# A mixture-of-experts layer on one core: the expert loop written out, new table steps, a second z3T buffer and a reordered last stage

## The reference, cut to what matters

```python
h = gelu(x[:, 1:] @ W1 + x[:, :1] @ W2 + b)          # 16 x 255 rows of 256
h = h + attention(layernorm(h))                       # 16 heads of 64
z = layernorm(h)
probs = softmax(z @ router_w);  topw, topi = top_k(probs, 2)      # 8 experts
routed = sum over the two experts e of  topw * (silu(z @ w1[e]) @ w2[e])
shared = sigmoid(z @ gate_w) * ((silu(z @ gate) * (z @ up)) @ down)
out = h + routed + shared
```

## Time and profile before

| | us |
|---|---|
| median of 3 runs | 1132.4 (1131.16 to 1133.53) |
| the profiled execution | 1139.81 |
| its span | 1138.0 |
| PE busy in the span | 1062.1 |
| DVE busy | 768.7 |
| POOL busy | 537.2 |

### The profile page before, as it was taken

How to read it: one execution, slowest core, us unless ns; L and a number is a source line. 1 busy time by engine, 2 the same in 40 slices (tenths; PEclk the granted TensorE clock), 3 DMA queues, 4 the chain that set the end, 5 groups by cost and what they waited for, 6 DMA issues and landing times.

```text
span 1138.0 us, 24005 instructions
## 1 busy us (share of the span) xinstructions
PE 1062.1 (93%) x8058; PEld 891.3 (78%) x8059; DVE 768.7 (68%) x1975; ACT 671.1 (59%) x2062; POOL 537.2 (47%) x575
## 2 busy tenths in 40 slices
PE   7979999999999999999999999999979798899985
PEld 6857788878877887877788788788858687898874
DVE  3757766785776678577667857766765954566666
ACT  4647765774775677477567747766774333454431
POOL 0025434554556455464545546454361746544542
PEclk9989999999999999999999999999999988999997
DMA  8110000000001000000100000010025423343494
GB/s 259 56 43 2 1 1 19 2 11 30 20 2 38 20 1 13 27 20 2 38 20 1 20 20 20 1 39 20 2 98 194 134 70 108 112 134 121 131 330 141
DMA packets 46624, 66.07 MB, mean 58 GB/s; under 512 B 7992, under 2 KB 39608, under 8 KB 45496
## 3 DMA queue, kind: packets, MB, share of 16 engines
q1 hardware_dynamic: 39720, 46.73, 13.1%
q0 software_dynamic: 6528, 17.97, 4.3%
q10 hardware_dynamic: 272, 0.00, 0.0%
HBM read 36.22 MB, written 28.46 MB: 57 GB/s over the span
## 4 chain that ended last, share of the span: by engine, by line
PE 72%; DVE 8%; issue 6%; POOL 5%; ACT 2%; another core or an unknown queue 1%; DMA 0%; DVEq 0%; SPq 0%; ACTq 0%; POOLq 0%
PE pT_ps L730 10%; PE o_ps L743 9%; PE proj_ps L68 9%; PE proj_ps L70 9%; PE proj_ps L69 9%; PE s_ps L716 8%; PE v_ps L68 2%; POOL prob L1676 2%; PE v_ps L69 2%; PE v_ps L70 2%; PE s_ps L68 2%; POOL prob L1678 2%; PE s_ps L70 2%; PE pT_ps L977 2%; PE s_ps L69 2%
## 5 line engine op out<-in xcount | busy, mean ns | idle before, releaser
L1039 ACT ACTIVATE prob<-s_ps,nmax 128x255 f32<-128x255 f32 x512 | 239.1, 478 | 227.7 <-DVE nmax L1251 227.6
L1676 POOL TENSOR_SCALAR prob<-prob,rinv 128x255 f32<-128x255 f32 x128 | 139.6, 1090 | 373.8 <-DVE rinv L1269 369.4
L1251 DVE TENSOR_REDUCE nmax<-s_ps 128x2 f32<-128x510 f32 x256 | 166.0, 681 | 37.9 <-PE s_ps L716 36.4
L730 PEld LDWEIGHTS pT_ps<-ident,prob 128*128 128x128 f32 x1024 | 109.8, 141 | 60.6 <-issue 49.7
L730 PE MATMUL pT_ps<-ident,prob 128*128 128x128 f32 x1024 | 146.2, 281 | 6.5 <-POOL prob L1678 3.4
L743 PE MATMUL o_ps<-probT,v 128*64 128x256 f32 x1024 | 139.6, 394 | 1.2 <-DVE oT_lo L1282 1.2
L1276 DVE COPY probT<-pT_ps 128x512 f32<-128x512 f32 x128 | 88.4, 691 | 77.0 <-PE pT_ps L730 77.0
L716 PE MATMUL s_ps<-qk_space 64*128 64x256 f32 x1536 | 125.2, 295 | 5.1 <-ACT prob L1039 4.4
L1678 POOL TENSOR_SCALAR prob<-prob,rinv 128x255 f32<-128x255 f32 x128 | 119.1, 931 | 0.0
L716 PEld LDWEIGHTS s_ps<-qk_space 64*128 64x128 f32 x1536 | 98.9, 185 | 21.8 <-issue 8.5
L1771 POOL DMA_INDIRECT expert_out_rows<-yg,y_at x72 | 69.4, 964 | 81.1 <-DVE yg L1581 45.4
(11 more groups left out here) (267 smaller groups left out, 2778.2 us busy)
## 6 DMA issues: line engine op xcount, KB each, us to landing
xg<-expert_in_rows SPq DMA_DIRECT2D x72, 130.0 KB
back<-expert_out_rows SPq DMA_DIRECT2D x8, 1024.0 KB, 9.4
xin<-in_x_dram SPq DMA_DIRECT2D x8, 512.0 KB, 4.4
z_rows<-z SPq DMA_DIRECT2D x8, 512.0 KB, 3.2
z<-z_rows SPq DMA_DIRECT2D x8, 512.0 KB
expert_in_rows<-bo_row SPq DMA_DIRECT2D x16, 128.0 KB
raw_up<-in_L_ffn_w_dram SPq DMA_DIRECT2D x8, 256.0 KB, 5.0
raw_down<-in_L_ffn_w_dram SPq DMA_DIRECT2D x8, 256.0 KB, 6.3
```

Of the source, the lines that this page charges most:

```text
L730: m = pe.transpose(pT_ps[h][:, o:o + P], prob[u_par(i)][:, h, qt, kt * P:(kt + 1) * P], ident[:])
L1039: m = act.activation(prob[u_par(i)][:, h, qt, 1:N], s_ps[h][:, qt * N + 1:(qt + 1) * N], ACT.Exp, bias=nmax[u_par(i)][:, n:n + 1], accum_o ...
L1251: dve.tensor_reduce(nmax[u_par(i)][:, 2 * h:2 * h + 2], s_ps[h][:].rearrange("p (q k) -> p q k", q=2)[:, :, 1:N], AX_X, ALU.max, negate=Tr ...
L1676: pool.tensor_scalar(prob[k][:, 0, 1, 1:N], prob[k][:, 0, 1, 1:N], rinv[k][:, 1:2], None, ALU.mult).then_inc(s_nA1, 1)
```

## The change

- `RUN` = 71 tiles in place of 72, and the whole expert loop is written out on all engines: no `Fori`, every semaphore value is a constant.
- The running sum `ends` (one copy and seven adds, each waiting for the one before) becomes one multiplication by a constant mask of 8x8 and one reduction. The mask `not_behind` is built on DVE at the start of the second stage.
- POOL waits for the tables (`s_table`) before its first `split_lo`. `hidden_split_lo` of groups 1, 2 and 3 moves from POOL to DVE; DVE's order around the tables changes.
- Two buffers for the transposed z3: `transpose_z3(g+1)` stands between the halves of `hidden(g)`, and ACT and DVE follow that order.
- In the last stage POOL no longer adds pairs: DVE adds twice for every group. `add_shared(6)` stands ahead of `add_experts(7)`. All eight `load_back` are issued ahead of the first store.
- PE's wait for `add_shared(3)` moves from before tile 0's turn to before the first `down_rows`.

```diff
+RUN = TOP * ROWS // P + E - 1
...
-        z3T_hi, z3T_lo = (over(n, qkv_at, 2 * part + k * half, [DC, GR], F32R) for k, n in enumerate(("z3T_hi", "z3T_lo")))
+        z3T_hi = [over("z3T_hi0", qkv_at, 2 * part, [DC, GR], F32R), over("z3T_hi1", qkv_at, 4 * part + half, [DC, GR], F32R)]
+        z3T_lo = [over("z3T_lo0", qkv_at, 2 * part + half, [DC, GR], F32R), over("z3T_lo1", at["probT1"], 0, [DC, GR], F32R)]
...
-            def load_x(r, k, first):
-
-                n = UNROLL * r + k
-                if not first:
+            def load_x(n):
+                if n >= BUFS:
                     sp.wait_ge(s_yc, n - BUFS + 1)
-                at = sp.value_load(tile_in[0:1, bass.ds(n, 1)], min_val=0, max_val=E * CAP + (SPARE - 1) * P)
-                sp.dma_start(xg[k % BUFS][:], x_slots[bass.ds(at, P), :]).then_inc(s_x_in[k % BUFS], 16)
-
-            def turn(r, last):
-                for k in range(UNROLL):
-                    if k + BUFS < UNROLL or not last:
-                        load_x(r + (k + BUFS) // UNROLL, (k + BUFS) % UNROLL, False)
+                at = sp.value_load(tile_in[0:1, n:n + 1], min_val=0, max_val=E * CAP + (SPARE - 1) * P)
+                sp.dma_start(xg[n % BUFS][:], x_slots[bass.ds(at, P), :]).then_inc(s_x_in[n % BUFS], 16)
...
-            for k in range(BUFS):
-                load_x(0, k, True)
-            for k in range(UNROLL):
-                load_x((k + BUFS) // UNROLL, (k + BUFS) % UNROLL, False)
-            with sp.Fori(1, TURNS - 1) as r:
-                turn(r, False)
-            turn(TURNS - 1, True)
+            for n in range(RUN):
+                load_x(n)
 
 
             load_z3(SHARED_EARLY + 2)
-            for k in range(UNROLL):
...
-            for g in range(2, 5):
+            for g in range(2, GROUPS):
                 load_back(g)
             for g in range(GROUPS):
                 store_group(g)
-                if g + 5 < GROUPS:
...
                 hidden(g, 0)
-                hidden(g, 1)
                 if g + 1 < SHARED_EARLY:
                     transpose_z3(g + 1)
+                hidden(g, 1)
...
-            transpose_x(0, 0)
-            transpose_x(0, 1)
+            transpose_x(0)
+            transpose_x(1)
             pe.wait_ge(s_table, TABLE_STEPS)
             pe.wait_ge(s_prod, FC * SHARED_EARLY)
-            up(0, 0, experts_of(0, 0)[0])
-            pe.wait_ge(s_added, 2 * SHARED_EARLY)
-            turn(0, True, False)
-            with pe.Fori(1, TURNS - 1) as r:
-                turn(r, False, False)
-            last_expert = turn(TURNS - 1, False, True)
+            e = experts_of(0)
+            up(0, e[0])
+            for n in range(RUN):
+                if n and n % HALF == 0:
+                    e = experts_of(n // HALF)
+                transpose_h(n)
+                if n + 2 < RUN:
+                    transpose_x(n + 2)
+                if n + 1 < RUN:
+                    up(n + 1, e[n + 1])
+                if n == 1:
+                    pe.wait_ge(s_added, 2 * SHARED_EARLY)
+                if n > 0:
+                    down_rows(n - 1, e[n - 1])
 
 
             transpose_z3(SHARED_EARLY)
-            down_rows(TURNS - 1, UNROLL - 1, last_expert)
+            down_rows(RUN - 1, e[RUN - 1])
...
             split_hi(1)
             silu(2, 0)
+            z3_hi(3)
+            hidden_split_hi(2, 0)
+            silu(2, 1)
+            hidden_split_hi(2, 1)
             split_hi(2)
-            silu(2, 1)
-            hidden_split_hi(2, 0)
-            z3_hi(3)
-            hidden_split_hi(2, 1)
+            silu(3, 0)
             split_hi(3)
-            silu(3, 0)
+            hidden_split_hi(3, 0)
             silu(3, 1)
...
-            def gated(r, k, first):
-                n = UNROLL * r + k
+                act.activation(xgT_hi[n % 2][:], xT_ps[n % 2][:, 0:DC * P], ACT.Copy).then_inc(s_xh, 1)
+
+            def gated(n):
                 act.wait_ge(s_up, n + 1)
-                if not first:
+                if n >= 2:
                     act.wait_ge(s_hT, n - 1)
-                act.activation(hg[k % 2][:], hg_ps[k % 2][:, 0:F], ACT.Silu).then_inc(s_h, 1)
-
-            def hidden_hi(r, k, first):
-                n = UNROLL * r + k
+                act.activation(hg[n % 2][:], hg_ps[n % 2][:, 0:F], ACT.Silu).then_inc(s_h, 1)
...
             z3_hi(SHARED_EARLY)
             for g in range(SHARED_EARLY, GROUPS):
                 silu(g, 0)
-                silu(g, 1)
-                hidden_split_hi(g, 0)
                 if g + 1 < GROUPS:
                     z3_hi(g + 1)
+                hidden_split_hi(g, 0)
+                silu(g, 1)
...
-                done(dve.tensor_copy(ends[:, 0:1], tiles_f[0:1, 0:1]))
-                for e in range(1, E):
-                    done(dve.tensor_tensor(ends[:, e:e + 1], ends[:, e - 1:e], tiles_f[0:1, e:e + 1], ALU.add))
+                done(dve.tensor_tensor(upto[:], not_behind[:], tiles_f[0:1].unsqueeze(1).broadcast_to([1, E, E]), ALU.mult))
+                done(dve.tensor_reduce(ends[:], upto[:], AX_X, ALU.add))
...
+            def hidden_split_lo(g):
+                for c in range(FC):
+                    dve.wait_ge(s_hhi, FC * g + c + 1)
+                    dve.tensor_tensor(h_lo[g % 2][:, c, :], h_full[:, c, :], f32(h_hi[g % 2][:, c, :]),
+                                      ALU.subtract).then_inc(s_hlo, 1)
...
+            dve.wait_ge(s_iota, 1)
+            dve.tensor_tensor(not_behind[:], iota[0:1].unsqueeze(2).broadcast_to([1, E, E]),
+                              iota[0:1].unsqueeze(1).broadcast_to([1, E, E]), ALU.is_ge)
...
             expert_ends()
+            dve.wait_ge(s_hlo, FC)
+            hidden_split_lo(1)
+            turns_past()
             add_shared(0)
             product(2, 0)
-            turns_past()
-            product(2, 1)
             z3_lo(3)
             tile_words()
+            product(2, 1)
+            hidden_split_lo(2)
             add_shared(1)
             product(3, 0)
             product(3, 1)
+            hidden_split_lo(3)
             add_shared(2)
             add_shared(3)
 
-            def x_lo(r, k):
...
-                if g in PAIRED_BY_POOL:
-                    dve.wait_ge(s_pair, PAIRED_BY_POOL.index(g) + 1)
-                else:
-                    dve.tensor_tensor(rows, rows, back[g][:, :, 1, :], ALU.add).then_inc(s_first, 1)
-                    dve.wait_ge(s_first, g + 1 - sum(n < g for n in PAIRED_BY_POOL))
+                dve.tensor_tensor(rows, rows, back[g][:, :, 1, :], ALU.add).then_inc(s_first, 1)
+                dve.wait_ge(s_first, g + 1)
...
             z3_lo(4)
             product(4, 0)
+            z3_lo(5)
             product(4, 1)
-            z3_lo(5)
             add_experts(0)
             product(5, 0)
-            product(5, 1)
             z3_lo(6)
             add_experts(1)
+            product(5, 1)
             add_experts(2)
+            product(6, 0)
+            z3_lo(7)
             add_shared(4)
-            product(6, 0)
             add_experts(3)
             product(6, 1)
-            z3_lo(7)
             add_experts(4)
+            product(7, 0)
             add_shared(5)
-            product(7, 0)
             add_experts(5)
             product(7, 1)
             add_experts(6)
+            add_shared(6)
             add_experts(7)
-            add_shared(6)
             add_shared(7)
 
         @block.gpsimd
@@ -1751,47 +1714,27 @@
             router_step(GROUPS, 1)
             router_step(GROUPS, 4)
             hidden_split_lo(0)
...
-            for t in range(2):
+            for t in range(GT):
                 router_step(GROUPS, UNITS - GT + t)
-            hidden_split_lo(1)
-            for t in range(2, GT):
-                router_step(GROUPS, UNITS - GT + t)
-            split_lo(0)
-            hidden_split_lo(2)
-            split_lo(1)
-            split_lo(2)
-            hidden_split_lo(3)
-            split_lo(3)
-
-            def scatter(r, k):
-                n = UNROLL * r + k
+            pool.wait_ge(s_table, TABLE_STEPS)
+            for e in range(HI_BY_SCALAR):
+                split_lo(e)
...
-            between = {(0, 3): 4, (0, 7): 5, (0, 11): 6, (1, 5): 7}
-            for r in range(2):
-                for k in range(UNROLL):
-                    scatter(r, k)
-                    if (r, k) in between:
-                        split_both(between[r, k])
-            with pool.Fori(2, TURNS) as r:
-                for k in range(UNROLL):
-                    scatter(r, k)
-
...
+            split_behind = {3: 4, 7: 5, 11: 6, 17: 7}
+            for n in range(RUN):
+                scatter(n)
+                if n in split_behind:
+                    split_both(split_behind[n])
+
+            for g in range(SHARED_EARLY, GROUPS):
+                hidden_split_lo(g)
 
```

(67 more changed lines are left out.)

119 lines of the change are left out of this document (43 added, 76 removed).

## The result

| | us |
|---|---|
| before, median of 9 runs | 1133.53 |
| after, median | 1125.86 (1122.83 to 1128.48) |
| ratio after / before | 0.9934, 95% interval 0.9916 to 0.9952 |
| predicted | 1115.1, range 1103 to 1123 |

The change saves 7.5 us where I predicted 17.3. The sign was right; the range missed by 2.9 us. (One execution of after took 4938 us: the ratio leaves it out, and without it the median is 1125.4.) The profiled execution took 1124.56 us, span 1122.8.

What follows compares the result with a forecast made beforehand. PE is busy 93% overall; behind attention, DVE kept out by POOL (tables), stalls above PE's 1.94 us a tile (loop) and DVE's additions (last stage) were blamed. Median: 1132.4 - 0.3 - 9.1 - 7.9 = 1115.1 us, range 1103 to 1123.

Steps and rivals of the forecast that it cites:

- 9.1 us for the median: Expert loop: saving forecast for the median run, 12.8 us less 3.7 for the long profiled execution.
- the 16.2 us of stalls: Expert loop: rest of the 19.0 us lost against the floor, at the loop's entry, in its first pass, less later.
- the middle between 4.7 and 20.9: Expert loop: 12.8 us taken for the profiled execution, between the sure saving and all stalls going.
- the stalls stay: Expert loop rival: stalls come from the word loads and stay, only 4.7 us saved, 1119.5 us; chance 0.15.
- Its 4.7 us: Expert loop: sure saving, 1.94 us for one tile less and 2.8 us for no branch or register arithmetic.
- the rival of a slower kernel: Expert loop rival: written-out code starves for instructions, 4.5 us a stall, up to 1155.7 us; chance 0.08.
- The forecast for the profiled execution: Whole kernel: 1139.8 - 0.3 - 12.8 - 7.9 = 1118.8 us.
- the predicted 7.9: Last stage: z3T waits go, DVE's additions bind, the end comes at 1126.4 against 1134.3; saves 7.9 us.
- 0.3 us predicted: Tables: ready 9.8 us earlier, but nearly all given back behind them; 0.3 us kept, bounds 0 and 8.
- The stall of 7 us on `hidden_split_lo(2)`: Behind the tables: DVE kept out until POOL's six queued subtractions end at 904.9; about 7 us.
- the second rival: Tables: DVE gets in after one of POOL's operations; 4.4 us kept, 1111 us; chance 0.12.
- my replay: Tables: DVE's steps replayed from the last z3_lo at 885.4, tables ready at 897.4 instead of 907.2.

Runs made afterwards that it cites:

- e3: Changed kernel with the expert loop as before (72 tiles, hardware loop on all engines): 1126.54 us, ratio to before 0.9933, chip 2.
- e5: e4 with POOL made to issue its scatters in bursts of four through the whole loop: 1155.24 us, ratio to before 1.0184, chip 11.
- e6: Changed kernel with the 16 operations of split_both(4..7) put one behind each of scatters 3 to 18: 1116.41 us, ratio to before 0.9830, chip 11.
- e4: Changed kernel with POOL's split_both of experts 4 to 7 moved ahead of its first scatter: 1115.41 us, ratio to before 0.9837, chip 2.
- e16: The changed kernel itself, run again on chip 2: 1126.76 us, ratio to before 0.9906.
- e1: Changed kernel with the last stage's orders, POOL's pair adds and load order as before: 1132.28 us, ratio to before 0.9970, chip 2.
- e2: Changed kernel with the tables' part as before (seven adds, POOL's hidden splits, no hold, early orders): 1127.39 us, ratio to before 0.9924, chip 2.
- e9: e4 without POOL's wait for the tables ahead of split_lo(0): 1111.08 us, ratio to before 0.9874, chip 4.
- e18: e9 again on chip 12: 1112.12 us, ratio to before 0.9873.
- e11: e5 with only a quarter of each row scattered: 1109.25 us, ratio to before 0.9856, chip 4.
- e13: e5 again on chip 2: 1168.29 us, ratio to before 1.0265.
- e7: Kernel before with split_both(4..7) moved ahead of the first scatter and nothing else changed: 1131.81 us, ratio to before 0.9970, chip 11.
- e15: e11 again on chip 2: 1168.18 us, ratio to before 1.0276.
- e14: e5 with a POOL memset behind each scatter, spacing them by 1.46 us, on chip 2: 1149.02 us, ratio to before 1.0121.

## Why the prediction was off

**Loop: the failed step.** I had 9.1 us for the median; undoing the part moved it by -0.2 (e3). The step that failed is the one that put the 16.2 us of stalls down to the loop by half ("at the loop's entry, in its first pass") and took the middle between 4.7 and 20.9. The stall at tile 10 stood right ahead of the `Fori`, but also right behind `split_both(5)`, and POOL's timeline, which I had not read there, shows the burst. e5 and e6 settle it for chips of that kind: bursts without splitting stall, splitting without bursts doesn't, and taking both away (e4) gives 11.4 us. The rival "the stalls stay" was right in what happens and wrong in its cause (the word loads; e4 keeps them). Its 4.7 us, a tile and the branches, are borne out by the traces, with 1.87 us for most tiles and 2.7 to 2.9 for the turns' edges, where I had 1.94 and 2.8. They aren't in the medians: e3 is 0.2 us under e16 and has the ratio of after in the result (0.9933 and 0.9934, each known to 0.2%). What offsets them is open; the stalls at tiles 12 to 24 differ between e3, e16 and after.

By the Trainium skill (Runtime: NRT & Kernel Launch, "Instruction fetch mechanics") a taken branch stalls when its target isn't held. The edges at tiles 37 and 49 cost 0.7 us each with no instruction packet on its way, so they don't show such a stall. Fetching the longer code costs nothing visible, as I had it: queue q8 brought 12 packets in the loop of after (I had reckoned nine) and 6 in that of before, and e4, with 12 as well, has none of the stalls at tiles 10 to 24. So the rival of a slower kernel failed.

**The profiled execution.** It was 7.4 us above the median, and I took half of it off. The trace of after is 1.3 us under its median, so the traces differ by 15.2 us and the medians by 7.7. The forecast for the profiled execution was 1118.8 and is 5.8 us off, that for the median 10.8.

**Last stage: right mechanism, and the price within the error.** By the traces 8.8 us (62.6 - 53.8) for the predicted 7.9, and 9.4 on chip 2 (63.8 in e1 against 54.4 in e16). DVE's stretch from the first addition to the end of `add_shared(6)` took 32.8 us (1081.36 to 1114.16) for 33.4, with five additions lengthened by POOL instead of four; the end behind it took 5.6 us and not 6.4. In the medians of chip 2 undoing it costs 5.5 us, by the ratios 3 to 12 us (0.9970 against 0.9906). These don't contradict the traces.

**Tables: the sum right by luck.** 0.3 us predicted; 0.3 by the traces, 0.6 by e2. Two errors cancel. The stall of 7 us on `hidden_split_lo(2)` didn't come; the second rival's lock, an operation each, is what the rows show. The four moved halves still took 6.1 us where they could take 2.6, and `shared_rows(3)` waits for `add_shared(2)` behind them. And the tables were ready 2.5 us later than predicted, since `z3_lo(3)` waited for ACT, which had stood "remote" for 3.12 and 2.25 us (at 891.91 and 894.76) beside the dispatch's eight indirect DMAs in a row, which the change itself had put together. On chips 4 and 12, where ACT doesn't stand there, the tables of held kernels are ready 14.2 us behind the dispatch's first DMA; my replay had 14.4, and after has 16.5. Tile 0 comes there after 32.9 to 33.1 us, 2.7 us earlier than in before's trace: more than I had, and less than the rival's 4.4. The two kernels without the hold (e9, e18) take 33.4 and 31.9 there, so on those chips the hold costs nothing that shows.

## What to carry to other kernels

When a stall stands beside the edge of a loop, read every engine's timeline in that stretch before giving it to the edge: here it was GpSimd's row of scatters, three or four back to back, and moving the splits ahead of the loop (e4) won more (11.4 us) than the whole change (7.5). An engine with slack should be kept from falling behind and catching up in indirect DMAs, so spread its other work over the loop or put it ahead. Taking work of an engine away can make a burst as well, as it did in the dispatch. And repeat an experiment that overturns a theory beside its control on one chip: e11 alone would have given the wrong cause.

The best of what ran: e4 and e6 on chips 2 and 11 (ratios 0.984 and 0.983), e9 on chips 4 and 12 (0.987 twice). e4 and e6 beat both kernels there. e9 beats before; after itself was never run on chips 4 or 12, so what the change is worth on them isn't known, and e9 wasn't run on chips 2 or 11. What is left in their loops is PE's waiting for the tiles' loads: seven waits and 4.6 us on `o_ps` in e18.

## What the runs showed of the hardware

The same program behaves differently from one kind of chip to another. During three or more indirect DMAs issued 1.27 us apart, ACT and DVE stood with no releaser named for up to 3.8 us in the loop (2.7 on average on `yg` in e5) on chips 2 and 11, and not on chips 4 and 12. All twelve traces from the two former have such waits (after has them too, 4 on `yg`; e13 16; e4 one on `hg` and two in the dispatch), and all six from the two latter have none at all. Chip 2 was used at two times and the others once each, so that it is the chip, and not what else stood at that time, is likely and not shown.

The dispatch shows it as well: with eight indirect DMAs in a row every trace of chips 2 and 11 has such a wait of 3.1 to 6.0 us on `z3T_hi`, and with two rows of four (e2 and e7, and before) none has. ACT there in e4 (chip 2), then in e9 (chip 4):

```profile
889.26 0.60 ACT L1092 ACTIVATE z3T_hi<-v_ps 128x512 fp32r<-128x512 f32 x1 [3.20 <-remote]
892.11 0.60 ACT L1092 ACTIVATE z3T_hi<-o_ps 128x512 fp32r<-128x512 f32 x1 [2.25 <-remote]
```

```profile
887.18 0.60 ACT L1092 ACTIVATE z3T_hi<-v_ps 128x512 fp32r<-128x512 f32 x1 [0.72 <-PE v_ps L850]
887.68 0.59 ACT L1092 ACTIVATE z3T_hi<-o_ps 128x512 fp32r<-128x512 f32 x1
```

It doesn't depend on the bytes (e15), and spacing softens it (e14). Whether PE's semaphore arrives late or its product ends late isn't settled: the ends of matmuls are modelled, and nothing else in the trace marks them.

DVE and POOL kept each other out in two ways. Two-operand subtractions of 128x512 took turns with POOL's (2.97 us for two), while the 1x78 `tensor_scalar` of before stood until the last of POOL's six had ended (6.95 us), and one 1x1 addition of two operands over both of POOL's subtractions (3.09 us). So it isn't the count of operands; no run put one form in the other's place, and what decides is open.
